# An attention and FFN block on one core: a third of the long probability tiles transposed by DMA

## The reference, cut to what matters

```python
def _L0_xattn_ref(query, key, value):           # causal, chunks of 512, running maximum
    scores = einsum('bhqd,bhkd->bhqk', q, kj) * SCALE        # SCALE = 64 ** -0.5
    scores = where(causal, -inf, scores)
    out = softmax(scores) @ v                                # kept up over the chunks
def _L0_ffn_ref(input, pweight, nweight, exps, bexps, mask_weight, scale, pbias, nbias, biasscale):
    soft = sigmoid(pweight) - sigmoid(nweight)               # [1024, 1024, 4]
    weight = einsum('oin,n->oi', soft, exps * sigmoid(mask_weight)) * scale[0]
    bias = quantised(einsum('on,n->o', pbias - nbias, bexps)) * biasscale[0]
    return einsum('bsi,oi->bso', input, weight) + bias
x = x + _L0_xattn_ref(layernorm(x), ctx, ctx)
x = x + _L0_ffn_ref(layernorm(x), ...)
```

## Time and profile before

| | us |
|---|---|
| median of three runs | 1277.84 |
| the profiled execution | 1274.72 |
| its span in the profile | 1272.9 |
| TensorE matmul busy | 1166.4 (92%) |
| VectorE busy | 1034.5 (81%) |
| ScalarE busy | 928.5 (73%) |
| GpSimd busy | 597.1 (47%) |

### The profile page before, as it was taken

The page is one execution under the profiler, slowest core; times in us unless marked ns, Lnnn a source line. Parts: engine busy times, 40 slices in busy tenths (PEclk is TensorE's granted clock), DMA queues, the critical chain, the costliest instruction groups (busy, mean ns, idle before and its releaser), DMA issues.

```text
span 1272.9 us, 29189 instructions
## 1 busy us (share of the span) xinstructions
PE 1166.4 (92%) x11376; PEld 883.3 (69%) x11376; DVE 1034.5 (81%) x1593; ACT 928.5 (73%) x2019; POOL 597.1 (47%) x717
## 2 busy tenths in 40 slices
PE   0677788999999999999999999999999999999998
PEld 0666675677777677777776677787786677777763
DVE  4576677888898888888897888888988888888872
ACT  2688876777877777787777777777787787777750
POOL 3399865433324954433325853333237844332241
PEclk9888899999999999999999999999999999999999
DMA  8979843543224955433316764444326755220112
GB/s 220 305 242 309 296 133 80 127 98 79 68 84 82 203 133 123 90 90 70 97 51 138 166 144 102 103 82 100 67 68 150 169 131 117 67 68 19 35 34 66
DMA packets 228984, 152.92 MB, mean 120 GB/s; under 512 B 204272, under 2 KB 204272, under 8 KB 228848
## 3 DMA queue, kind: packets, MB, share of 16 engines
q1 hardware_dynamic: 227264, 148.92, 47.2%
q10 hardware_dynamic: 1584, 2.14, 0.5%
HBM read 67.15 MB, written 16.78 MB: 66 GB/s over the span
## 4 chain that ended last, share of the span: by engine, by line
PE 63%; DVE 15%; POOL 6%; issue 5%; ACT 5%; DMA 4%; SPq 2%; ACTq 1%; POOLq 0%
PE ffnb L399 19%; PE ptb L367 15%; PE oacc L381 7%; PE slot L354 7%; PE slot L355 7%; DVE pt_lo L561 5%; PE oacc L383 4%; DVE stats L575 4%; POOL v L758 3%; ACT pt_hi L461 2%; DVE mx L554 2%; PE slot L358 2%; DVE ring L610 1%; ACT osb L468 1%; DMA yt<-in_L_ffn_nweight_dram 1%
## 5 line engine op out<-in xcount | busy, mean ns | idle before, releaser
L561 DVE SCALAR_TENSOR_TENSOR pt_lo<-ptb,pt_hi 128x384 f16<-128x384 f32 (+2 forms) x688 | 382.8, 597 | 119.7 <-ACT pt_hi L461 117.5
L461 ACT ACTIVATE pt_hi<-ptb 128x384 f16<-128x384 f32 (+2 forms) x688 | 326.4, 527 | 166.2 <-PE ptb L367 165.5
L451 ACT ACTIVATE p<-slot,mx 128x512 f32<-128x512 f32 (+7 forms) x512 | 378.5, 748 | 52.1 <-DVE mx L554 50.0
L399 PE MATMUL ffnb<-wt,yt 128*128 128x512 f16 x1464 | 371.0, 379 | 19.7 <-DVE ring L610 17.9
L554 DVE TENSOR_REDUCE mx<-slot 128x1 f32<-128x640 f32 (+7 forms) x352 | 359.4, 1021 | 21.3 <-PE slot L358 18.6
L367 PE MATMUL ptb<-id,p 128*128 128x128 f32 x2304 | 323.7, 279 | 11.1 <-DVE pt_lo L561 10.0
L354 PE MATMUL slot<-kt,qt 128*128 128x128 f16 (+3 forms) x1056 | 270.5, 286 | 32.6 <-DMA qs<-qt 28.0
L743 POOL TENSOR_TENSOR att<-osb 128x256 f32<-128x256 f32 x128 | 99.1, 774 | 421.9 <-ACT osb L468 397.7
L355 PE MATMUL slot<-kt,qs 128*128 128x128 f16 (+3 forms) x1056 | 270.0, 285 | 0.0
L367 PEld LDWEIGHTS ptb<-id,p 128*128 128x128 f32 x2304 | 246.3, 141 | 18.2 <-issue 15.7
L381 PE MATMUL oacc<-v,pt_hi 128*128 128x128 f16 x2304 | 244.2, 220 | 3.6 <-DVE pt_lo L561 1.9
(11 more groups left out here) (78 smaller groups left out, 1064.6 us busy)
## 6 DMA issues: line engine op xcount, KB each, us to landing
ring<-in_x_dram SPq DMA_DIRECT2D x32, 512.0 KB, 4.9
cin<-in_ctx_dram SPq DMA_DIRECT2D x32, 512.0 KB, 4.0
qs<-qt SPq DMA_DIRECT2D x64, 256.0 KB, 3.9
out_dram<-ring SPq DMA_DIRECT2D x32, 512.0 KB, 2.9
v<-in_L_ffn_pweight_dram SPq DMA_DIRECT2D x20, 512.0 KB, 7.0
kt<-in_L_ffn_nweight_dram SPq DMA_DIRECT2D x15, 512.0 KB, 7.7
kt<-in_L_ffn_pweight_dram SPq DMA_DIRECT2D x5, 512.0 KB, 5.1
ring<-in_L_ffn_pweight_dram SPq DMA_DIRECT2D x5, 512.0 KB, 5.4
```

The source lines that it names most:

```text
L399: last = pe.matmul(dst, yt[:, k % 2, a * KT_N + kk, :], wt[:, c, kk, half * 512:half * 512 + 512], start=r == 0, stop=r == 3 * KT_N - 1)
L451: last = nc.scalar.activation(p32[:, j.par, hh * j.keys:(hh + 1) * j.keys], slot[:, j.par, base:base + j.keys], ACT.Exp, bias=mx[:, j.par, ...
L461: nc.scalar.activation(pt_hi[:, j.par, P * blocks.start:P * blocks.stop], ptb[:, c % 2, 0:P * len(blocks)], ACT.Copy, scale=P_SCALE).then_ ...
L561: nc.vector.scalar_tensor_tensor(pt_lo[:, j.par, cols], ptb[:, c % 2, 0:P * len(blocks)], P_SCALE, pt_hi[:, j.par, cols], ALU.mult, ALU.su ...
```

## The change

Jobs of one head with `q % 3 == 2` (q is the job's number in its tile: 2, 5, 8, 11 and 14 of the long tiles, 80 jobs in all) have a number `d` and no chunks. Their probabilities are not transposed by TensorE. ScalarE copies them, scaled and rounded to f16, from `p32` to `p16` directly behind their exponential; VectorE writes the low part beside it; SyncE asks for one DMA transpose of both into a place of its own, `ptd`; the values are computed from there. `pt_hi` and `pt_lo` are now one tile `pt`. The memory comes from `spare32`, whose place `p16` takes, and from `qs`, which has one place instead of two and is swapped in two halves. In tiles of 8 and 16 steps from tile 4 on, the low parts of y, context and q are computed on GpSimd instead of VectorE. The moments of the next y come behind the FFN result in VectorE's step, and the transpose of the keys stands at step 9 of most long tiles instead of the last.

```diff
+        self.d = turned if self.heads == 1 and q % 3 == 2 else None
+        count = -(-blocks // 4) if self.d is None else 0
...
+SWAP = {4: (0, 2), 8: (2, 6), 16: (6, 14)}
...
+def turn_k_step(t):
+    return 9 if steps(t) == 16 and t % NT < NT - 1 else steps(t) - 1
+def low_on_pool(t):
+    return t > 3 and steps(t) > 4
...
+            def turn_p(j):
+                sp.wait_ge(p16_lo, j.d + 1)
+                if j.d > 0:
+                    sp.wait_ge(pv_done, TURNED[j.d - 1].n + 1)
+                sp.dma_start_transpose(ptd[:, 0:2 * j.blocks], p16[:, 0:2 * j.keys]).then_inc(pt_in, 16)
...
                 for s in range(n):
+                    if s + 1 < n and JOBS[FIRST[t] + s + 1].d is not None:
+                        turn_p(JOBS[FIRST[t] + s + 1])
...
             def values(j):
-                pe.wait_ge(lo_done, j.chunks[-1][0] + 1)
+                if j.d is None:
+                    pe.wait_ge(lo_done, j.chunks[-1][0] + 1)
+                else:
+                    pe.wait_ge(pt_in, 16 * (j.d + 1))
...
             def exponentials(j):
                 act.wait_ge(mx_ready, j.n + 1)
+                if j.n > 1 and JOBS[j.n - 2].d is not None:
+                    act.wait_ge(p16_lo, JOBS[j.n - 2].d + 1)
...
+                if j.d is not None:
+                    act.wait_ge(p_done, j.n + 1)
+                    reached(act, pt_in, 16 * j.d)
+                    nc.scalar.activation(p16[:, 0:j.keys], p32[:, j.par, 0:j.keys], ACT.Copy, scale=P_SCALE
+                                         ).then_inc(p16_hi, 1)
...
+            def low_part_unturned(j):
+                dve.wait_ge(p16_hi, j.d + 1)
+                nc.vector.scalar_tensor_tensor(p16[:, j.keys:2 * j.keys], p32[:, j.par, 0:j.keys], P_SCALE,
+                                               p16[:, 0:j.keys], ALU.mult, ALU.subtract).then_inc(p16_lo, 1)
...
                     weights_low(j.n - 1)
+                if j.n + 1 < len(JOBS) and JOBS[j.n + 1].d is not None:
+                    low_part_unturned(JOBS[j.n + 1])
                 if j.n + 2 < len(JOBS):
                     maxima(JOBS[j.n + 2])
...
-                for k in y_begun(t, s):
-                    y_moments(k)
                 for k, m0, m1 in matmuls_at(t, s):
                     for half in range(2):
                         if m0 < MATMULS // 2 * (half + 1) <= m1:
                             result(k, half)
+                for k in y_begun(t, s):
+                    y_moments(k)
...
+                if low_on_pool(t):
+                    for k in y_at(t, s, 2):
+                        y_split(k)
+                    if s == C_LO[steps(t)] and t + 2 < TILES:
+                        c_split(t + 2)
+                    if q_at(t, s, 3):
+                        q_split(t + 2)
```

More of the change, by code:

```diff
@@ L44, with __init__ @@
 class Job:
-    def __init__(self, n, t, q, chunk0):
+    def __init__(self, n, t, q, chunk0, turned):
         self.n, self.t, self.q = n, t, q
@@ L66 @@
     for _q in range(H // HPJ[_t % NT]):
-        JOBS.append(Job(len(JOBS), _t, _q, JOBS[-1].chunks[-1][0] + 1 if JOBS else 0))
+        JOBS.append(Job(len(JOBS), _t, _q, sum(len(j.chunks) for j in JOBS), sum(j.d is not None for j in JOBS)))
 FIRST.append(len(JOBS))
+TURNED = [j for j in JOBS if j.d is not None]
 LAST_OF_GROUP = [j.n for j in JOBS if j.closes_group]
@@ L166, in build @@
         ring = sb("ring", [P, RING, DM], F32)
-        spare32 = sb("spare32", [P, DM], F32)
+        p16 = sb("p16", [P, 2 * 8 * P], F16)
         cin = sb("cin", [P, DM], F32)
@@ L295, in _ @@
             turn_q(0)
-            swap_q(0)
+            swap_q(0, 0)
+            swap_q(0, 1)
             load_w(2)
@@ L354, in scores @@
                         pe.matmul(dst, qt[:, t % 2, h, :], keys, start=True, stop=False, skip_group_check=True)
-                        last = pe.matmul(dst, qs[:, t % 2, h, :], keys, start=False, stop=end <= i,
+                        last = pe.matmul(dst, qs[:, h, :], keys, start=False, stop=end <= i,
                                          skip_group_check=True)
@@ L680, in _ @@
                     weights_sum(j.n + 1)
-                for k in y_at(t, s, 2):
-                    y_split(k)
-                if s == C_LO[steps(t)] and t + 2 < TILES:
-                    c_split(t + 2)
+                if not low_on_pool(t):
+                    for k in y_at(t, s, 2):
+                        y_split(k)
+                    if s == C_LO[steps(t)] and t + 2 < TILES:
+                        c_split(t + 2)
                 if q_at(t, s, 0):
                     q_moments(t + 2)
-                if q_at(t, s, 3):
+                if not low_on_pool(t) and q_at(t, s, 3):
                     q_split(t + 2)
-                for k in y_begun(t, s):
-                    y_moments(k)
                 for k, m0, m1 in matmuls_at(t, s):
```

76 lines of the change are left out of this document (49 added, 27 removed).

## The result

The changed kernel takes 1309.91 us (median of 4 runs, 1307.72 to 1317.67) against 1277.51 for the kernel before on the same chip: a ratio of 1.0268, interval 1.0245 to 1.029. It is slower by 32 us in the medians and by 35 in the two profiled executions, where I forecast 6, and the time lies 2 us above my range. The profiled execution has a span of 1308.4 us (1272.9 before).

A forecast was written before the change was run, and what follows sets the result against it. TensorE was taken to bound the kernel, VectorE and ScalarE only 10 to 20% behind. 19 - 5 - 8 = +6 on the profiled 1274.72 us gives about 1280; the median lies 3 above: 1283.5 us, range 1243 to 1308.

The forecast's parts named there:

- the round over VectorE and ScalarE: In long tiles, three steps can't be shorter than a serial loop over both engines: 9.11 us (8 blocks), 6.23 (5).
- Rival C: TensorE stays the bound because the loop is looser than added up: 1200 us (1180 to 1240); chance 0.12.
- the port: VectorE's low parts 11 and 8 wait for GpSimd at a locked SBUF port: 1.3 to 2.3 and 0.6 to 0.85 us.
- Rival B: Loop without lock: VectorE's low part slips past GpSimd, 40 us less, some taken up elsewhere: 1256 us; chance 0.23.
- the DMA at 0: The DMA transposes of turned probabilities land before the values need them, so their transfer costs 0.
- Rival D: DMA transposes land late and values wait on TensorE: 1343 us, or 1308 if only two jobs a tile; chance 0.15.
- the sum by tile, +19: Over the 16 long tiles: +2.6 us with 8 blocks, -0.2 with 5, mean +1.2, together 19 us more.
- A fall of TensorE's clock is no case of its own.: In long tiles the granted clock was taken to stay at 1.00, despite waits of 3 to 4 us behind job 11.
- The middle tiles lie between, mean +1.2: The 6- and 7-block long tiles were placed between -0.2 us (5 blocks) and +2.6 (8 blocks).
- -8 for the result first: The FFN result ahead of the next tile's moments saves 8 us of TensorE's 17.9 us of waits (bounds 0 and -18).
- -5: Four closing intervals of long tiles run into a short tile without turned jobs: 5 us less.
- the forecast's own case: The changed kernel ends within 1276 to 1300 us; chance 0.50.

The follow-up runs named there:

- e3: Changed kernel with VectorE's maximum of job j+2 moved ahead of the new low part of job j+1: 1264.58 us, ratio 0.9915.
- e4: Changed kernel with GpSimd's long-tile bias addition in step 2 instead of 9 and q's subtraction in step 13 instead of 11: 1293.14 us, ratio 1.0133.
- e8: Changed kernel plus eight 512-column matmuls on zeros behind step 11's FFN matmuls in 6-, 7- and 8-block tiles: 1305.09 us, ratio 1.0237.
- e10: Kernel before the change with only the FFN result put ahead of the next norm's sums in VectorE's step: 1277.35 us, ratio 1.0023.
- e13: Changed kernel with the next norm's sums put back ahead of the FFN result in all tiles: 1310.26 us.
- e2: Changed kernel with no job turned by DMA, everything else of the change kept: 1262.15 us, ratio 0.9895.
- e9b: Changed kernel, but from the second batch on ScalarE copies only the first 128 columns of a turned job's high part: 1275.22 us, ratio 0.9995.
- e1: Changed kernel with the low parts of y, context and q back on VectorE in every tile: 1307.77 us, ratio 1.0254.

## Why the prediction was wrong in size

**Right: the round over VectorE and ScalarE.** I forecast 9.11 us for three steps, and 2.03 and the port wait more behind job 8. From the maximum behind low part 8 to the one behind low part 11 the 8-block tile shows 12.48 us (666.98 to 679.46); my number was 9.11 + 2.03 + 1.3 = 12.4, and its terms are there one by one: the FFN result 0.60, q's cast and the output copy 1.43, the port 1.27. From low part 5 to 8 it is 9.81, where I had 9.11 + 0.6 = 9.7, but that is luck. My 0.6 was a wait for the port, and low part 8 was not held (1.23 us); instead the high parts waited for TensorE's transposes and the exponential for the context's cast, 0.7 us together. The copy was taken at 1.06 and measured 1.06, the low part at 1.15 and takes 1.14 to the next start. e3 opens the round and gets 45 us. Rival C (no round) fell.

**Right: the port, where it was met.** Low part 11 takes 2.50 us, started 1.42 us ahead of the end of GpSimd's addition, and ends 1.08 behind it, as in the earlier trace rows. By the Trainium skill's rule ("SBUF — State Buffer", section "SBUF: two separate sides") the lock holds for the whole instruction and either side can be the one that waits. The trace agrees: q's subtraction, behind the addition, took 3.10 us where free ones take 2.12 to 2.14, and v's 3.15 at 665.90, beside the low part that began at 665.84. Rival B (no lock) fell; e4 prices the meeting at 17 us over 12 tiles. But with 5 blocks I had 2.3 + 0.85 = 3.15 us of it, and there neither low part was held (0.83 us each). Other work filled the gap, so that this tile's sum came out right by luck.

**Right: the DMA at 0.** 2.3 us of waits in 4 places, 4.0 us to landing in the median. Rival D would have given 1308, nearly the measured time, by a cause that is not there.

**Wrong: the sum by tile, +19.** This is the term that failed. From low part 2 to the next tile's low part 2 (with 8 blocks to low part 14 only) the 16 long tiles took 725.9 us, where my numbers, with a line between the two outer tiles, give 695.4: 30 us over, which is the whole miss. The table has the pieces, in us; "without a fall" is a tile of the changed kernel, from batch 2 or 3, with no fall of the clock, with 8 blocks that of e8.

| blocks | 5 | 6 | 7 | 8 |
|---|---|---|---|---|
| free round, forecast | 6.23 | 7.19 | 8.15 | 9.11 |
| free round, measured (e4) | 6.53 | 7.41 | 8.41 | 9.30 |
| port waits, forecast | 3.15 | 2.7 | 2.3 | 1.9 |
| port waits, measured | 0 | 2.8 | 2.0 | 1.3 |
| low part 2 to 14, forecast | 30.3 | 33.7 | 37.1 | 40.5 |
| the same, without a fall | 29.8 | 35.4 | 38.2 | 40.9 |
| 14 to the next tile's 2, forecast | 9.6 | 10.8 | 12.0 | |
| the same, without a fall | 10.5 | 11.6 | 12.8 | |

Two steps of the prediction stand behind the 30 us.

- *"A fall of TensorE's clock is no case of its own."* I had worked out waits of 3 to 4 us for TensorE behind job 11, seen that the trace of before had none so long, and still priced them at their own length. The eight falls made their tiles 0.4 to 1.5 us longer than tiles of the same size without one, some 10 us in all. e8 fills the stop in the 8-block tile, keeps the clock and gets 1.2 to 1.5 us there.
- *"The middle tiles lie between, mean +1.2", and the round on either side of them.* Some 20 us are left without the clock, most of it, about 16, in the 6- and 7-block tiles. It is not the port, which I had about right there. Every free round is 0.19 to 0.30 us longer than I added it, an estimated 16 us over 64 rounds; in the 8-block tile 0.13 of it is between the exponential and the high parts behind it. The interval from one tile to the next is 0.8 to 0.9 over, some 10 us in 12 tiles, and the tile's other work on the round some 0.3 to 1.5 a tile. The port waits that did not come hid some 16 us of this. Why the closing intervals are long I can't say from these runs.

**Wrong in its place: -8 for the result first.** The short tiles did win, some 2 us a batch in e10, but the long ones paid for it, which my sum had at nothing; e10 shows no time left of it in all, and e13 none in the changed kernel's. That the remainder of the account still came out at -14 against my -5 - 8 = -13 is luck in part: e2 shows the first batch's short tiles 6.3 us shorter with nothing turned, by the rest of the change, where I had 0 and e10 shows no gain.

My chance for the forecast's own case rested on a mechanism that was right; the range was too narrow above it.

## What to carry to other kernels

When work leaves a full engine, write down the cycle that the other engines then form, instruction by instruction, and look at the order in the instruction streams first: the low part at the head of VectorE's step cost 45 us more than the same work behind one maximum. Where a wait of a few microseconds for TensorE is part of a forecast, add what the clock may take behind it, and read a wait off more than one tile, since the same wait had a fall in one tile and none in the next. A round added up from single durations came out 2 to 5% short here, which counts when it runs 64 times. A producer that comes a little sooner can run into a lock that it missed before, so price meetings on a shared port place by place, and don't take the sum of a wait in a list as time to be won: look at each kind of tile for who pays it back.

## What the runs showed of the hardware

- Idle of 2.53 us on TensorE was followed by a granted clock of 0.50 for 3.4 us; with eight idle matmuls (1.89 us) in it the clock stayed at 1.00, and the tile got 1.5 us shorter with more work. Not each such stop does it: 2.71 us in the 7-block tile of the same batch were followed by 1.00, and in batch 4 a stop of 2.27 us in the 6-block tile was followed by a fall.
- The port between VectorE and GpSimd excludes in both directions. A held low part of 1024 columns ended 1.06 to 1.08 us behind the end of what it met, the bias addition (the changed kernel, e9b), the context's subtraction (e3) or the normalisation (e9b); GpSimd's normalisation, which reads one large tile (1.20 us when free), took 2.24 beside a low part in e1 (rows below, GpSimd and VectorE), so not only two-input instructions of GpSimd are held.

```profile
665.03 2.24 POOL L771 TENSOR_SCALAR norm<-ring,rstd 128x1024 f32<-128x1024 f32 x1
```
```profile
665.05 1.22 DVE L611 SCALAR_TENSOR_TENSOR p<-p 128x1024 f16<-128x1024 f32 x1 [0.26 <-ACT p L498]
```

- SBUF-to-SBUF transposes of 320 to 512 KB land in 4.0 us in the median at five a tile; at seven a tile ScalarE waited 120.2 us in all for their one place, although their median landing was the same 4.0.
